# Two unread runs of products lengthened at the start of a softmax attention, and a group's first stack transfers issued ahead of the rows with its maxima

## The chip, the cores and the metric

The kernel runs on one core of one Trainium2 chip. The metric is the device time of one execution in microseconds (us), given as the median of three runs. TensorE is called PE below, VectorE DVE, ScalarE ACT, GpSimd POOL and SyncE SP; SP issues the transfers that this text is about.

## The reference, cut to what matters

One layer is computed: softmax attention, a small feed-forward network, a linear attention over time, and the same network again, each on the layer norm of the running sum. The change touches the first part alone.

```
x:     4 sequences x 512 tokens x 256 channels
mixed  = layernorm(x) @ Wqkv.T         # 16 heads of 16 channels, q, k and v
attn   = softmax(q @ k.T / 4)          # 512 x 512 for each of 4 x 16 pairs
ctx    = attn @ v
x      = x + ctx @ Wproj.T + bproj
```

## The kernel before

The first part works in eight groups: a group is one sequence and half of the heads (8 heads). A group has eight chunks, in two quads: a quad is four heads, and a chunk is one block of 128 keys for the four heads of a quad. PE, ACT and DVE each follow a list of slots written out by hand; slot c of group s is position 8s + c, and there are 70 slots.

What happens to a group, with the lines that do it:

- **Projection.** PE projects q and k of group s + 1 (L373) during slots 1 to 3 of group s. ACT copies the upper parts to `a_dense` (L589) and DVE writes what is left over to it (L679), w = 0 in slot 2 and w = 1 in slot 3.
- **Restacking.** `restack(g, quad)` on SP moves `a_dense` into `a_stack` (L305): three parts, two transfers each, so six transfers of 128 KB a quad. Its first two wait for ACT's copy, the other four for DVE's.
- **Maxima.** PE computes the scores of group s once (L417, four products a slot), and DVE takes each row's negated maximum (L697). After the fourth slot of a quad DVE splits the maxima in two parts, PE turns them (L394, `transpose_max`), ACT copies them (L629), and SP writes them as two more rows of the stack (`rows(g, quad)`, L316, four transfers of 4 KB).
- **Probabilities.** Six slots later PE computes the scores again, turned, with the maxima inside the product (L440, four products a slot), ACT takes the exponentials (L616), and PE multiplies them by the values (L456, `context`). The first L440 of a quad waits for its maxima's rows (`max_rows`), and the first L417 of a quad for its stack (`stacked`).

So in slot c = 4 the maxima of quad 0 of group s are copied, and in slot c = 6 its first L440 needs the rows. In slot c = 0 of the next group the first L417 needs the first quad of that group's stack. SP issues all transfers in the order of its program, and waits at each for what that one needs. The stack has two buffers, so group s + 1 writes where group s - 1 was read.

`unread(count)` on PE (L423) issues products of 128x512 into the accumulator `a_ctx_acc` that nobody reads; the first real product into it starts it afresh. Before the change there are three such runs, all in group 0: six in slot 2, two in slot 4 ahead of `transpose_max`, two in slot 6 ahead of the first L440.

After the softmax part the others follow one after another, so what moves its end moves the end of the kernel.

Of the kernel before, what the change touches and what calls it, by code (L numbers as in the profile page):

```python
# [150 lines left out]
def softmax_attention(nc, semaphore, x, w_qkv, w_stack, loads, bias_rows, x_tok, xn_hi, xn_lo, ident, ctx_tok, norm_tiles):  # L151
# [10 lines left out]
    groups = NB * KD  # L162
# [8 lines left out]
    with ExitStack() as ctx:  # L171
# [111 lines left out]
        @block.sync  # L283
        def _(sp):
            for b in range(NB):
                sp.dma_start(x_tok[:, b * TPB:(b + 1) * TPB, :],
                             x[b].rearrange("(t p) d -> p t d", p=P)).then_inc(x_loaded[b], 16)
                if b == 0:
                    sp.dma_start(stack_raw, w_stack).then_inc(stack_w_loaded, 16)
                    sp.dma_start(w_raw, w_qkv).then_inc(w_qkv_loaded, 16)  # L290
            for dst, src in loads:
                sp.dma_start(dst, src).then_inc(w_loaded, 16)
            sp.wait_ge(set_up, 2)

            def restack(g, quad):

                i, hs = g % 2, slice(quad * 2, quad * 2 + 2)
                if g >= 2:

                    sp.wait_ge(scores_t_done, 4 * ((g - 2) * chunks + (quad + 1) * TPB))  # L300
                for r, (k_part, q_part) in enumerate(((K_HI, Q_HI), (K_LO, Q_HI), (K_HI, Q_LO))):
                    sp.wait_ge(dense_lo_done if r else dense_hi_done, 2 * g + 2)
                    for e in range(2):
                        at, of = e * HALF_ROWS + r * HN, quad * 4 * HN + e * 2 * HN
                        sp.dma_start(f32(stack[i][at:at + HN, hs, :, :]),  # L305
                                     f32(dense[of:of + 2 * HN, i, k_part:q_part + 1:q_part - k_part, :])).then_inc(
                            stacked[i][quad], 16)

            def rows(g, quad):

                i = g % 2
                sp.wait_ge(max_copied, quads * g + quad + 1)
                for e in range(2):
                    for pair in range(2):
                        at, of = e * HALF_ROWS + STACK, (2 * e + pair) * 2 * TPB
                        sp.dma_start(f32(stack[i][at:at + 2, 2 * quad + pair, 1, :]),  # L316
                                     f32(max_rows_t[of:of + 2 * TPB, quad, :])).then_inc(max_rows[quad], 16)

            restack(0, 1)
            for s in range(groups + 1):  # L320
                if s >= 1:
                    rows(s - 1, 1)
                if s < groups:
                    rows(s, 0)
                if s + 1 < groups:
                    restack(s + 1, 0)
                    restack(s + 1, 1)
            sp.wait_ge(w_loaded, 16 * len(loads))

# [26 lines left out]
        def _(pe):  # L356
# [63 lines left out]
            def unread(count):  # L420

                for _ in range(count):
                    pe.matmul(ctx_acc[:], w_hi[:, 0, 0:P], xn_hi[:, 0, 0:SEQ], start=True, stop=True)  # L423

            def probs_chunk(g, c, half):

                quad, t, i = c // TPB, c % TPB, g % 2
                n = g * chunks + c
                if n == 0 and half == 0:
                    unread(2)  # L430
                if t == 0 and half == 0:
                    pe.wait_ge(max_rows[quad], 64 * (g + 1))
                slot = quad * 2 + half
                for e in range(2):
                    q = 4 * n + 2 * half + e
                    if q < TURNS:
                        pe.wait_ge(max_done, last_wide(TURNS + q) + 1)
                    else:
                        pe.wait_ge(probs_done, q - TURNS + 1)
                    pe.matmul(scores_t[q % TURNS][:], half_rows(k_stack[i], e, STACK + 2)[:, slot, t * P:(t + 1) * P],  # L440
                              half_rows(q_stack[i], e, STACK + 2)[:, slot, :], start=True,
                              stop=True).then_inc(scores_t_done, 1)
# [17 lines left out]
            def after_context(s, c):  # L460

                projects, values = s + 1 < groups, s + 1 < groups and (s + 1) % KD == 0
                if c == 0 and s >= 1:
                    if s % KD == 0 and s < groups:
                        pe.wait_ge(v_copied, copied(s))
                    elif turned_in(s - 1):
                        pe.wait_ge(ln.lo_done, KD * (turned_in(s - 1) + 1))
                    else:
                        pe.wait_ge(ctx_done, quads * (s - 2) + 1)
                    transpose_max(s - 1, 1)  # L470
                elif c == 1 and projects:
                    if s >= 2:
                        pe.wait_ge(ctx_done, quads * (s - 1))
                    elif s == 1:
                        pe.wait_ge(max_copied, quads * s)
                    else:
                        pe.wait_ge(v_copied, 1)
                        for e in range(2):
                            project_values(0, 1, e)
                    if s >= 1:  # L480
                        project(s + 1, 0, 0)
                elif c == 0 and s == 0:
                    for k in range(KD):
                        project(0, 1, k)
                    for w in range(2):
                        project_stack(1, w)
                elif c == 3 and projects:
                    project(s + 1, 1, 1)
                elif c == 4 and s < groups:
                    if s == 0:  # L490
                        unread(2)
                    if projects:
                        pe.wait_ge(dense_lo_done, 2 * (s + 1) + 2)
                    else:
                        pe.wait_ge(ctx_done, quads * (s - 1))
                    transpose_max(s, 0)
                elif c == 5 and values:
                    pe.wait_ge(ctx_done, quads * (s - 1) + 1)
                    project_values((s + 1) // KD, 0, 0)
                elif c == 7 and values:  # L500
                    project_values((s + 1) // KD, 1, 1)
                elif c == 5 and turned_in(s):
                    if s >= 1:
                        pe.wait_ge(ctx_done, quads * (s - 1) + 1)
                    else:
                        pe.wait_ge(max_copied, 1)
                    pe.wait_ge(ln.normed, (turned_in(s) + 1) * TPB)
                    ln.turn(pe, turned_in(s), 0, misc)
# [49 lines left out]
            for slot in range(groups * chunks + lag):  # L558
                s, c, n = slot // chunks, slot % chunks, slot - lag
# [1405 lines left out]
```

## Time and profile before

| what | value |
|---|---|
| median of three runs | 1193.58 us (1189.43 to 1196.62) |
| profiled execution, its own time | 1196.9 us |
| its span | 1195.1 us |
| PE busy | 1136.5 us, 95% of the span |
| DVE busy | 930.0 us, 78% |
| ACT busy | 773.7 us, 65% |
| granted clock of PE, mean | 0.975 |

The softmax part takes about the first 276 us of the span. PE's busy share is high, but a product's end is modelled, and at half of the clock the same products are busy for longer. So what counts is where PE stood still, what ended that, and which clock was granted. The granted clock has two levels here: 1.00 is 2.4 GHz and 0.50 is 1.2 GHz.

### The profile page before, as it was taken

What the parts mean: (1) busy time and instruction counts of PE and PEld (TensorE: products, weight loads), DVE (VectorE), ACT (ScalarE), POOL (GpSimd) and SP (SyncE); (2) the same over time, 40 slices, a digit from 0 to 9 for tenths busy, and PEclk for the clock granted to TensorE, in tenths of its full rate; (3) what the DMA queues carried; (4) which work ended last, traced back from release to release, by engine and by line L of the source; (5) the groups of instructions that cost most, each with busy time, mean ns of one, the idle gap of its engine ahead of it and who ended that gap; (6) DMA issues with size and microseconds to landing.
All of it is one profiled execution on the core that took longest, in us unless ns stands there. A gap on an engine that the chain in (4) does not pass through costs nothing. (4 is left out here: it accounts for less than half of the span.)

```text
span 1195.1 us, 22426 instructions
## 1 busy us (share of the span) xinstructions
PE 1136.5 (95%) x7548; PEld 909.1 (76%) x7548; DVE 930.0 (78%) x2126; ACT 773.7 (65%) x1535; POOL 636.8 (53%) x1077
## 2 busy tenths in 40 slices
PE   8899999888898899999999999999999999999768
PEld 7443434336666899999999999999999999999646
DVE  6888877855557988888888888888888888888552
ACT  3377766773456676777776777777777777676423
POOL 4020500000614876777786777686777687767520
PEclk9799989998998999999999999999999999999889
DMA  6434434400320111112111211211211201111020
GB/s 181 55 55 55 55 54 55 54 2 1 113 69 20 34 48 67 47 33 82 34 46 37 78 39 41 76 38 44 71 45 35 82 33 46 33 47 33 16 70 1
DMA packets 23449, 60.50 MB, mean 51 GB/s; under 512 B 3367, under 2 KB 8359, under 8 KB 22183
## 3 DMA queue, kind: packets, MB, share of 16 engines
q1 hardware_dynamic: 23335, 59.07, 19.0%
q8 instruction: 61, 1.00, 0.4%
q14 instruction: 53, 0.43, 0.1%
HBM read 44.67 MB, written 2.33 MB: 39 GB/s over the span
## 5 line engine op out<-in xcount | busy, mean ns | idle before, releaser
L1722 DVE SCALAR_TENSOR_TENSOR ln_xn<-l_proj_q,par,ln_xn 128x511 f32<-128x511 f32 (+2 forms) x192 | 142.4, 742 | 99.4 <-ACT ln_xn L1621 97.1
L697 DVE TENSOR_REDUCE a_neg_max<-a_scores 128x1 f32<-128x512 f32 x244 | 155.1, 683 | 39.9 <-PE a_scores L417 38.1
L616 ACT ACTIVATE a_probs<-a_scores_t 128x512 f32<-128x512 f32 x256 | 138.3, 599 | 65.1 <-PE a_scores_t L440 64.2
L1627 ACT ACTIVATE ln_xn<-ln_xn,par 128x512 f32<-128x512 f32 x128 | 92.6, 724 | 94.0 <-DVE ln_xn L1722 94.0
L1378 POOL TENSOR_TENSOR l_k_tok<-l_normed,k_norm 128x384 f32<-128x384 f32 x64 | 65.2, 1018 | 158.6 <-ACT l_normed L1638 158.6
L1722 DVE SCALAR_TENSOR_TENSOR ln_xn<-l_proj_k,par,ln_xn 128x511 f32<-128x511 f32 (+2 forms) x192 | 142.9, 744 | 4.5
L1638 ACT ACTIVATE l_normed<-l_turn_q,l_shift,l_scale 128x128 f32<-128x128 f32 x256 | 96.5, 457 | 27.2 <-POOL l_shift L1370 27.2
L1368 POOL TENSOR_TENSOR l_scale<-l_small,l_minus_half 128x8 f32<-128x8 f32 x64 | 105.2, 1644 | 5.0
L1638 ACT ACTIVATE l_normed<-l_turn_k,l_shift,l_scale 128x128 f32<-128x128 f32 x256 | 97.4, 481 | 0.0
L1692 ACT ACTIVATE l_gate<-l_proj_gv 128x512 f32<-128x512 f32 x64 | 38.2, 597 | 80.1 <-PE l_proj_gv L1440 80.1
L1576 PE MATMUL l_outp<-l_masked,l_values 128*128 128x128 f32 x512 | 89.3, 277 | 0.1
L1408 POOL TENSOR_TENSOR l_gated_lo<-l_gated,l_gated_hi 128x512 fp32r<-128x512 f32 x64 | 83.3, 1302 | 9.3 <-ACT l_gated_hi L1661 9.3
L1729 DVE TENSOR_TENSOR_SCAN l_decay<-l_keep,ident 128x128 f32<-128x128 f32 x256 | 87.1, 403 | 0.0
L440 PE MATMUL a_scores_t<-a_stack 50*128 50x512 f32 x256 | 76.6, 510 | 9.1 <-ACT a_probs L616 5.0
L96 POOL TENSOR_SCALAR ln_var_eps<-ln_mean_var 128x4 f32<-128x4 f32 (+1 forms) x13 | 3.0, 233 | 152.9 <-DVE ln_mean_var L79 94.2
L440 PEld LDWEIGHTS a_scores_t<-a_stack 50*128 50x128 f32 x256 | 29.9, 192 | 64.9 <-ACT a_probs L616 39.7
L1604 PE MATMUL l_outp<-wo_hi,l_gated_hi 128*128 128x256 f32 x256 | 73.6, 288 | 5.5 <-DVE l_gated L1820 3.4
L1453 PE MATMUL l_proj_gv<-head_hi,xn_hi 128*128 128x256 f32 x256 | 76.5, 299 | 0.3 <-ACT l_gate L1692 0.3
L89 POOL MEMSET ln_minus_half<- 128x4 f32 (+1 forms) x4 | 0.4, 102 | 139.5 <-POOLq L171 139.4
L456 PE MATMUL a_ctx_acc<-a_probs,a_v_tok 128*32 128x512 f32 x512 | 72.5, 640 | 2.3 <-ACT a_probs L616 1.7
L1579 PE MATMUL l_outp<-l_q_late,l_state 128*128 128x128 f32 x384 | 74.5, 276 | 0.0
L1576 PEld LDWEIGHTS l_outp<-l_masked,l_values 128*128 128x128 f32 x512 | 73.3, 194 | 0.3 <-issue 0.3
(347 smaller groups left out, 3614.6 us busy)
## 6 DMA issues: line engine op xcount, KB each, us to landing
l_keep<-keep_rows SPq DMA_DIRECT2D x64, 448.0 KB, 3.6
a_stack<-a_dense SPq DMA_DIRECT2D x90, 128.0 KB, 5.1
head_raw<-w_heads SPq DMA_DIRECT2D x8, 1024.0 KB, 6.7
x_tok<-x SPq DMA_DIRECT2D x4, 512.0 KB, 8.3
wo_raw<-w_o SPq DMA_DIRECT2D x1, 2048.0 KB, 12.0
out<-x_tok SPq DMA_DIRECT2D x1, 1920.0 KB
a_stack<-a_max_rows_t SPq DMA_DIRECT2D x64, 4.0 KB
ctx_tok<-w_qkv SPq DMA_DIRECT2D x1, 768.0 KB, 6.9
```

The source lines that it names most:

```text
L440: pe.matmul(scores_t[q % TURNS][:], half_rows(k_stack[i], e, STACK + 2)[:, slot, t * P:(t + 1) * P], half_rows(q_stack[i], e, STACK + 2)[: ...
L616: act.activation(probs[:, n % 2, h, :], scores_t[(4 * n + h) % TURNS][:], ACT.Exp, scale=SOFT_SCALE).then_inc(probs_done, 1)
L697: dve.tensor_reduce(neg_max[:, g % 2, at:at + 1], max_bank(g, j), AX.X, ALU.max, negate=True).then_inc(max_done, 1)
L1368: pool.tensor_tensor(scale[:, i, :], small[:, 7, :], minus_half[:], ALU.pow).then_inc(scales_ready, 1)
L1408: pool.tensor_tensor(gated_lo[:, k % 4, :], gated[:], f32(gated_hi[:, k % 4, :]), ALU.subtract).then_inc(gated_lo_done, 1)
L1453: last = pe.matmul(proj_gv[:, t * PAIR:(t + 1) * PAIR], lhs, rhs, start=(j == 0), stop=(j == 3 * KD - 1))
L1576: last = pe.matmul(outp[:, tok], values[:, c % 2, t, e * DK:(e + 1) * DK], masked[:, m, tok], start=True, stop=(t == 0))
L1579: last = pe.matmul(outp[:, tok], state[:, m, t - 1, :], q_late[:, m, (t - 1) * P:t * P], start=False, stop=True)
L1627: act.activation(conv[:, w, m, :], conv[:, w, m, :], ACT.Silu, bias=par[:, h, 2 * TAPS + w:2 * TAPS + w + 1]).then_inc(act_sem[w], 1)
L1638: last = act.activation(normed[:, w, t, :], turn[w][:, t * P:(t + 1) * P], ACT.Identity, scale=scale[:, m, j:j + 1], bias=shift[:, m, j:j ...
L1722: ins = dve.scalar_tensor_tensor(conv[:, w, m, s:], proj[w][:, 0:SEQ - s], par[:, h, tap:tap + 1], conv[:, w, m, s:], ALU.mult, ALU.add)
L1729: last = dve.tensor_tensor_scan(decay[:, tok], keep[:, r, tok], ident[:], 0.0, ALU.mult, ALU.add)
```

## The change

The run of two unread products in slot 4 becomes a run of five, and that of two in slot 6 a run of ten. On SP, `restack(s + 1, 0)` of groups s = 1 to 6 is issued ahead of `rows(s, 0)` and no longer behind it. For s = 0 the order is as before. No transfer and no product that is read is added or removed.

```diff
             for s in range(groups + 1):
                 if s >= 1:
                     rows(s - 1, 1)
+                if s >= 1 and s + 1 < groups:
+                    restack(s + 1, 0)
                 if s < groups:
                     rows(s, 0)
+                if s == 0:
+                    restack(1, 0)
                 if s + 1 < groups:
-                    restack(s + 1, 0)
                     restack(s + 1, 1)
...
                 if n == 0 and half == 0:
-                    unread(2)
+                    unread(10)
...
                     if s == 0:
-                        unread(2)
+                        unread(5)
```

On SP the order at s = 1 was this before. `a_stack1<-a_max_rows_t` is `rows(1, 0)`, and `a_stack0<-a_dense` is the stack of group 2, first quad 0 and then quad 1.

```order
L316 DMA a_stack1<-a_max_rows_t 2x4x128 [waits a_max_copied]
L316 DMA a_stack1<-a_max_rows_t 2x4x128 x3
L305 DMA a_stack0<-a_dense 16x2x1024 [waits a_dense_hi_done,a_scores_t_done]
L305 DMA a_stack0<-a_dense 16x2x1024
L305 DMA a_stack0<-a_dense 16x4x512 [waits a_dense_lo_done]
L305 DMA a_stack0<-a_dense 16x4x512
L305 DMA a_stack0<-a_dense 16x4x512 [waits a_dense_lo_done]
L305 DMA a_stack0<-a_dense 16x4x512
```

And this is the same stretch of SP's program in the changed kernel.

```order
L305 DMA a_stack0<-a_dense 16x2x1024 [waits a_dense_hi_done,a_scores_t_done]
L305 DMA a_stack0<-a_dense 16x2x1024
L305 DMA a_stack0<-a_dense 16x4x512 [waits a_dense_lo_done]
L305 DMA a_stack0<-a_dense 16x4x512
L305 DMA a_stack0<-a_dense 16x4x512 [waits a_dense_lo_done]
L305 DMA a_stack0<-a_dense 16x4x512
L316 DMA a_stack1<-a_max_rows_t 2x4x128 [waits a_max_copied]
L316 DMA a_stack1<-a_max_rows_t 2x4x128 x3
```

Six stack transfers now stand between the copy of the dense parts and the four transfers of the rows; the same swap recurs for each s up to 6.

On PE the first lengthened run stood as follows, in slot 4 of group 0 ahead of the turning of the maxima (L394).

```order
L417 MATMUL a_scores_t1<-a_stack0 128x512 [waits a_max_done,a_stacked01]
L417 MATMUL a_scores_t2<-a_stack0 128x512 [waits a_max_done]
L417 MATMUL a_scores0<-a_stack0 128x512 [waits a_max_done]
L417 MATMUL a_scores1<-a_stack0 128x512 [waits a_max_done]
L423 MATMUL a_ctx_acc<-xn_hi,a_w_hi 128x512 x2
L394 MATMUL a_misc<-ident,a_max_parts 32x128 [waits a_max_split,a_dense_lo_done]
```

In the changed kernel three lines more stand ahead of `unread` in the file, and the count is five.

```order
L420 MATMUL a_scores_t1<-a_stack0 128x512 [waits a_max_done,a_stacked01]
L420 MATMUL a_scores_t2<-a_stack0 128x512 [waits a_max_done]
L420 MATMUL a_scores0<-a_stack0 128x512 [waits a_max_done]
L420 MATMUL a_scores1<-a_stack0 128x512 [waits a_max_done]
L426 MATMUL a_ctx_acc<-xn_hi,a_w_hi 128x512 x5
L397 MATMUL a_misc<-ident,a_max_parts 32x128 [waits a_max_split,a_dense_lo_done]
```

Only the run itself has grown; the run of ten grows in the same way ahead of the first L440.

## Rows read from the trace of the kernel before

**Rows 1.** The page: granted clock of PE in 40 slices of the span
```profile
PEclk9799989998998999999999999999999999999889
```

**Rows 2.** Windows: stretch, its length, busy us (instructions), PEclk, DMA share, GB/s
```profile
40.71:54.36 13.65, 12.71 (x45) 5.41 (x46) 9.48 (x18) 6.18 (x13) 0.00 (x0) 0.50 0.88 117
170.42:177.24 6.82, 6.82 (x28) 2.85 (x24) 3.67 (x7) 2.44 (x5) 0.00 (x0) 0.50 0.28 33
```

**Rows 3.** Timeline of PE, group 0: start, us, instruction [idle before <-releaser]
```profile
30.34 1.65 PE L423 MATMUL a_ctx_acc<-xn_hi,a_w_hi 128*128 128x512 f32 x6
...
37.13 0.28 PE L394 MATMUL a_misc<-ident,a_max_parts 128*32 128x128 f32 x1 [1.05 <-DVE a_dense L679]
...
39.17 0.71 PE L423 MATMUL a_ctx_acc<-xn_hi,a_w_hi 128*128 128x512 f32 x2
41.66 0.80 PE L440 MATMUL a_scores_t<-a_stack 50*128 50x512 f32 x2 [1.77 <-DMA a_stack<-a_max_rows_t]
...
50.02 1.21 PE L417 MATMUL a_scores<-a_stack 48*128 48x512 f32 x2
...
54.37 0.96 PE L440 MATMUL a_scores_t<-a_stack 50*128 50x512 f32 x2
```

**Rows 4.** Timeline, group 2, the stretch from its rows to its stack
```profile
96.63 0.60 ACT L589 ACTIVATE a_dense<-a_misc 128x512 fp32r<-128x512 f32 x1
...
98.88 2.57 SPq L316 DMA_DIRECT2D a_stack<-a_max_rows_t  x4
...
102.69 0.42 PE L440 MATMUL a_scores_t<-a_stack 50*128 50x512 f32 x1
...
103.31 0.50 PE L440 MATMUL a_scores_t<-a_stack 50*128 50x512 f32 x1 [0.20 <-ACT a_probs L616]
...
108.86 0.40 PE L440 MATMUL a_scores_t<-a_stack 50*128 50x512 f32 x1
...
109.93 0.67 PE L417 MATMUL a_scores<-a_stack 48*128 48x512 f32 x2
```

**Rows 5.** Timeline of PE, group 2, the slots behind that
```profile
113.01 0.50 PE L440 MATMUL a_scores_t<-a_stack 50*128 50x512 f32 x2
...
117.33 0.50 PE L440 MATMUL a_scores_t<-a_stack 50*128 50x512 f32 x2
```

**Rows 6.** Timeline of PE, group 4, the same slots as in group 2
```profile
167.00 0.39 PE L440 MATMUL a_scores_t<-a_stack 50*128 50x512 f32 x1
...
169.10 0.50 PE L417 MATMUL a_scores<-a_stack 48*128 48x512 f32 x2 [0.99 <-DMA a_stack<-a_dense]
...
179.06 0.50 PE L440 MATMUL a_scores_t<-a_stack 50*128 50x512 f32 x2
```

**Rows 7.** Timeline of SP's queue: runs of twelve stack transfers (two quads)
```profile
40.50 7.65 SPq L305 DMA_DIRECT2D a_stack<-a_dense  x12
...
159.68 8.68 SPq L305 DMA_DIRECT2D a_stack<-a_dense  x12
```

**Rows 8.** Timeline, group 6: rows issued with nothing of the stack ahead
```profile
218.74 2.57 SPq L316 DMA_DIRECT2D a_stack<-a_max_rows_t  x4
...
222.47 0.61 PE L440 MATMUL a_scores_t<-a_stack 50*128 50x512 f32 x2 [0.24 <-DMA a_stack<-a_max_rows_t]
```

**Rows 9.** Timeline, group 6 to 7: rows issued behind twelve stack transfers
```profile
229.79 0.50 PE L417 MATMUL a_scores<-a_stack 48*128 48x512 f32 x2 [0.57 <-DMA a_stack<-a_dense]
...
231.83 2.65 SPq L316 DMA_DIRECT2D a_stack<-a_max_rows_t  x4
...
236.03 0.50 PE L440 MATMUL a_scores_t<-a_stack 50*128 50x512 f32 x2 [0.76 <-DMA a_stack<-a_max_rows_t]
```

**Rows 10.** Timeline, group 1: the same chain in an odd group
```profile
67.05 0.60 ACT L589 ACTIVATE a_dense<-a_misc 128x512 fp32r<-128x512 f32 x1
...
69.29 2.55 SPq L316 DMA_DIRECT2D a_stack<-a_max_rows_t  x4
...
74.43 0.51 PE L440 MATMUL a_scores_t<-a_stack 50*128 50x512 f32 x2
```

## The prediction

> **What bounds the kernel now.** I read the granted clock over the whole span first. The page's line of the clock stays at 9 tenths but for a few slices, and the second is one of them, near the place of the lengthened runs [rows 1]. The windows then give the two stretches of the softmax part that matter here. From 40.71 to 54.36 us PE ran at 0.50 of its clock (1.2 GHz) for 13.65 us, and from 170.42 to 177.24 for 6.82 us; it was busy for 12.71 and 6.82 us of them, so these are stretches of work at half speed [rows 2].
>
> Next I read what PE did just before each. Before the first it stood still for 1.05 us ahead of the turning of the maxima and for 1.77 us ahead of the first L440, which waited for the rows of the maxima [rows 3]. Before the second it stood still for 0.99 us at the first L417 of group 5, which waited for its stack [rows 6]. A shorter wait of that kind, 0.57 us, opens group 7, and did not lower the clock [rows 9].
>
> Last I read the slack of the two kinds of transfers that trade places. In group 6 the four transfers of the rows are issued from 218.74 for 2.57 us, to 221.31, and the L440 that waits for them starts at 222.47: **they land 1.16 us after the end of their issue** [rows 8]. In group 2 the issue ends at 101.45 and the L440 starts at 102.69, 1.24 us later, so there they land with no slack [rows 4]. In group 1 the issue ends at 71.84, they land at 73.0, and L440 starts at 74.43: 1.4 us of slack [rows 10]. Groups 4 and 6 repeat group 2 and groups 3 and 5 repeat group 1. The stack has as little: in group 2 the issue of the rows ends at 101.45, the stack follows, and the first L417 starts at 109.93, about when it lands; the same wait cost 0.99 and 0.57 us two and four groups later [rows 4, 6, 9]. So at both places a transfer sets when PE goes on, and SP can serve only one first.
>
> **The longer runs.** Six unread products took 1.65 us, some 0.25 from one to the next once the tail of the last is left off [rows 3]. Three more in slot 4 are 0.75 us inside a wait of 1.05: they cost nothing, and if DVE were earlier by more than 0.3 us they would show. Eight more in slot 6: ten products from 39.17 at 0.25 take PE's issue to 41.67, and the rows let L440 go at 41.66 [rows 3]. I put the cost at 0.1 us; the bounds are nothing, and 0.25 us, one product. What they give is the clock: PE then works through both waits that came before the first fall, and I expect no fall there.
>
> What is that worth? From 41.66 to 54.37 are three slots, 12.71 us [rows 3]. The same three slots of group 2, 102.69 to 113.01, took 10.32 at 1.00, and hold one run of L456 more (about 1.0 us), so 9.3 [rows 4, 5]. But the full 3.4 us can't come back. The stack of group 1 is issued from 40.50, and in group 2 one issued from 101.45 let its L417 go at 109.93, 8.4 us later [rows 7, 4]. So the L417 that starts group 1 at 50.02 can't start before 48.9: 1.1 us. From there to the end of the slot it took 4.35 us (50.02 to 54.37) against 3.1 (109.93 to 113.01): 1.25 us. **Gain: 2.4 us**, between 0 (a fall at the new wait for that stack) and 3.4.
>
> **The swap on SP.** In groups 1 to 6 SP now starts on the stack when ACT has copied the dense part. Twelve such transfers are issued in 7.65 us, 0.64 each, or in 8.68 where the queue paused; the seven such runs lie between these two [rows 7]. Six take 3.8 us, then the rows 2.57, then 1.16 to land: 7.6 us from ACT's copy. Their own condition, the copy of the maxima, is met meanwhile (SP could start them at 98.88, 1.65 us after ACT's copy ended) [rows 4].
>
> - Even groups (2, 4, 6): ACT's copy ends at 97.23, so the rows land at 104.8 where L440 started at 102.69. **PE waits 2.1 us** [rows 4]. Three times: 6.3.
> - Odd groups (1, 3, 5): 67.65 + 7.6 = 75.25 against 74.43. **PE waits 0.8 us** [rows 10]. Three times: 2.4.
> - The pauses of the queue: up to 1.0 us more in a run of twelve [rows 7]. I take 0.2 a group, 1.2; bounds 0 and 2.4.
> - What comes back: behind the L440 that would wait, the next product starts 0.62 us after the first since it waits for ACT's exponentials, where 0.25 is the pace without a wait [rows 3, 4]. After a stall ACT has caught up, and the 0.4 us is not paid; the pair that begins at 108.86 waits in the same way. I take 0.6 us in each even group, 1.8, between 1.2 and 2.4. In the odd groups PE has no such waits, and nothing comes back.
> - The stack lands some 4 us earlier, so the waits of 0.99 and 0.57 us go: 1.6 gained [rows 6, 9]. The fall of the clock that followed the first goes too. It cost: 167.00 to 179.06 is 12.06 us, the same slots of group 2, 108.86 to 117.33, are 8.47; of the 3.6 us the wait is 1.0. **A fall of the clock costs 2.6 us**, and one is gained [rows 4 to 6].
> - New falls: the new waits of 2.1 us are longer than each of those before the two falls in rows (1.05 with 1.77, and 0.99), and 0.57 and 0.76 were followed by none [rows 2, 3, 6, 9]. So I expect the odd groups to keep the clock and the even ones to lose it mostly: two falls of three, 5.2 us; bounds 0 and 7.8.
>
> Who waits behind? On SP the second quad's stack follows, 1.7 us earlier than before, so nobody. On PE all of the slot waits, and ACT and DVE with it once they have done what is ready; hence the stall counts in full but for what came back above.
>
> The size hangs on one thing more. In rows 9 four transfers of rows were issued behind twelve of the stack, to 234.48, and let L440 go at 236.03, 1.55 us after and not 1.16 [rows 8, 9]. The Trainium skill, page "DMA: Bandwidth & Descriptors", section on queues, rings and completion order, says that on each DMA engine descriptors are taken in the order of the ring. By that the small rows must wait for the big transfers ahead of them to drain, and the 0.4 us agrees in sign.
>
> **The sum.** 0.1 + 6.3 + 2.4 + 1.2 - 1.8 - 1.6 - 2.6 + 5.2 - 2.4 = **+6.8 us**. Against the profiled execution's 1196.9 that is 1203.7. The median of the runs is 3.3 us lower than that execution, so on its scale the forecast is 1193.6 + 6.8 = 1200.4.
>
> **The rivals.**
> - *The clock holds.* The waits for the rows come as computed, but no fall follows them: 6.8 - 5.2 = +1.6 us, 1195.2. For it speaks that PE is busy on both sides of each wait; against it that 0.99 us was enough once.
> - *The queue holds the rows back.* If the rows land only after the sixth stack transfer, they come 8.4 us after its first issue and not 7.6; with that 0.8 us in six groups (4.8), and a third fall (2.6), it is +14.2, 1207.8. Rows 9 show 0.4 of it.
> - *Faster: the rows' wait is absorbed.* The wait replaces waiting that PE has later in the same group, for ACT and for the stack. In the even groups the two waits for ACT are 0.8 us and that for the stack up to 1.0; should the rows land 1.8 us or less after their old place, an even group loses nothing and an odd one nothing up to its 1.4 us. It then takes the stack to be issued faster, or DVE and ACT to set the pace. The gains are left: 2.4 + 2.6 + 1.6 = 6.6 us, 1187.0. From a landing 5.9 us after ACT's copy (odd groups 6.8), not 7.6, it decides.
> - *The runs don't keep the clock.* The first fall comes a little later, at the new wait for group 1's stack: +2.4 on the forecast, 1202.8.
>
> **How the numbers follow.** A measurement of this kernel can tell about 0.5% (6 us) from no change; its three runs spread over 7.2 us. Chances: forecast 0.40 (alone 1197 to 1205), clock holds 0.20, queue holds back 0.13, absorbed 0.20, first fall stays 0.07. Slower by more than 0.5% is above 1199.5: half and a little more of the forecast, all of the queue's case and most of the last, and some of the clock's, 0.45. Faster is under 1187.6: somewhat more than half of the absorbed case, with some from the clock's when another fall later is missing, 0.19. The rest is 0.36. The range of 1188 to 1208 leaves out half of the absorbed case and the upper half of the queue's.
>
> **What would show it.** Right: the runs of five and ten stand close to L397 and L443, and the clock is 1.00 from 37 to 48 us; in groups 1 to 6 the stack's first transfers start within 0.1 us of ACT's copy and the rows' issue 3.8 us later; L443 has waits for the rows of about 2 and 1 us in turn, no L420 waits for the stack but the first of group 1; stretches of 0.50 follow the even groups' waits. Wrong: the rows' waits are under 0.5 us; or they are there and the end of the softmax part has still moved forward; or the falls come at other places, so that their number is chance and the medians differ by it.

## The result, and the profile after

| | before | changed |
|---|---|---|
| median of 4 runs each | 1191.51 us (1186.12 to 1196.62) | 1217.74 us (1216.2 to 1226.04) |
| profiled execution, its own time | 1196.9 us | 1226.04 us |
| its span | 1195.1 us | 1224.2 us |
| granted clock of PE, mean | 0.975 | 0.955 |

The ratio is 1.023 with a 95% interval of 1.0171 to 1.0288. The kernel became slower by 26 us, where +6.8 was forecast; the time lies outside the range. The sign was right, the size was not. The profiled execution of the changed kernel is the slowest of its four and 8.3 us above their median, so the stretches at half clock below may add up to more than in the other three, which were not profiled.

The page of the changed kernel, its line of the clock and the row of its scores (the last number is the idle time that the rows of the maxima ended). What was L440 is now L443, L417 is L420, and L394 is L397.

```profile
PEclk9888899968899899999999999999999999999979
...
L443 PE MATMUL a_scores_t<-a_stack 50*128 50x512 f32 x256 | 80.6, 544 | 20.6 <-DMA a_stack<-a_max_rows_t 16.4
```

The line of the clock answers to [rows 1]. A slice is 30.6 us. In the softmax part, now ten slices long, the second to the fifth stand at 8 tenths, the ninth at 6 and the tenth at 8; in its nine slices before, the second stood at 7, the sixth at 8 and the rest at 9. PE's waits in 36 to 310 us say what was late (total us, times, longest):

```profile
PE a_scores_t L443 <- DMA a_stack<-a_max_rows_t: 16.4, 8, 3.7
...
PE a_scores L420 <- DMA a_stack<-a_dense: 1.3, 1, 1.3
```

In the same stretch before, the wait for the rows was 4.0 us in five. Here is one group after another, groups 1, 2 and 6 of the changed kernel, in the timeline. It answers to [rows 10, 4, 8].

```profile
65.61 0.61 ACT L592 ACTIVATE a_dense<-a_misc 128x512 fp32r<-128x512 f32 x1
...
66.29 3.80 SPq L305 DMA_DIRECT2D a_stack<-a_dense  x6
...
70.13 2.65 SPq L316 DMA_DIRECT2D a_stack<-a_max_rows_t  x4
...
74.91 0.49 PE L443 MATMUL a_scores_t<-a_stack 50*128 50x512 f32 x2 [1.85 <-DMA a_stack<-a_max_rows_t]
...
100.09 0.60 ACT L592 ACTIVATE a_dense<-a_misc 128x512 fp32r<-128x512 f32 x1
...
100.76 3.96 SPq L305 DMA_DIRECT2D a_stack<-a_dense  x6
...
104.77 2.66 SPq L316 DMA_DIRECT2D a_stack<-a_max_rows_t  x4
...
109.19 0.50 PE L443 MATMUL a_scores_t<-a_stack 50*128 50x512 f32 x2 [2.88 <-DMA a_stack<-a_max_rows_t]
...
236.35 0.60 ACT L592 ACTIVATE a_dense<-a_misc 128x512 fp32r<-128x512 f32 x1
...
245.75 0.80 PE L443 MATMUL a_scores_t<-a_stack 50*128 50x512 f32 x2 [3.66 <-DMA a_stack<-a_max_rows_t]
```

Read each as one chain. In group 2 ACT's copy ends at 100.69, SP starts at 100.76, the six stack transfers take 3.96 us, the rows 2.66, and the L443 that needs them starts 1.76 us after the end of their issue. From ACT's copy to L443 that is 8.5 us, in group 1 it is 8.7 (with 2.13 behind the issue), in group 6 8.8. The trace also has the moments of landing. In group 2 the sixth stack transfer lands at 108.58 and the rows at 109.15, and in all of groups 1 to 6 the rows land 0.6 to 0.8 us after that sixth transfer. The six waits of groups 1 to 6 are 1.85, 2.88, 1.93, 3.09, 1.67 and 3.66 us, 15.1 in all.

The windows of the changed kernel at half clock in that part (columns as in [rows 2], to which they answer), and the one ahead of the first:

```profile
36.00:49.49 13.49, 11.27 (x60) 5.65 (x59) 12.52 (x23) 6.57 (x13) 0.00 (x0) 1.00 0.67 92
49.49:56.31 6.82, 6.82 (x26) 2.73 (x24) 4.01 (x9) 2.34 (x5) 0.00 (x0) 0.50 0.47 56
76.79:83.62 6.83, 6.83 (x28) 3.50 (x26) 2.75 (x5) 2.95 (x7) 0.00 (x0) 0.50 0.45 60
110.93:127.99 17.06, 17.06 (x62) 6.59 (x64) 10.54 (x22) 7.66 (x15) 0.00 (x0) 0.50 0.19 26
148.47:155.30 6.83, 6.83 (x28) 3.59 (x28) 2.79 (x5) 2.99 (x7) 2.70 (x1) 0.50 0.41 49
182.61:189.43 6.82, 6.82 (x29) 2.74 (x25) 3.78 (x8) 3.74 (x8) 0.00 (x0) 0.50 0.52 72
244.05:264.53 20.48, 18.78 (x70) 6.81 (x70) 9.78 (x18) 8.38 (x17) 0.00 (x0) 0.50 0.27 40
```

Each from the second on begins 1.5 to 1.9 us behind the end of a wait for the rows (74.91, 109.19, 146.62, 181.14), the last already within it (ended 245.75); only group 5's wait, 1.67 us, has none behind it. Together they are 64.8 us at 0.50, against the 20.5 of [rows 2].

How the two traces drift apart is seen from the first scores product of each group's probabilities:

| group | 1 | 2 | 3 | 4 | 5 | 6 | 7 |
|---|---|---|---|---|---|---|---|
| before, us | 74.43 | 102.69 | 132.57 | 160.82 | 194.29 | 222.47 | 248.17 |
| changed, us | 74.91 | 109.19 | 146.62 | 181.14 | 214.15 | 245.75 | 277.39 |
| difference | 0.5 | 6.5 | 14.1 | 20.3 | 19.9 | 23.3 | 29.2 |
| changed, waits filled, us | 75.56 | 107.11 | 138.17 | 169.71 | 200.62 | 232.05 | 256.49 |

The last row belongs to an experiment below. The spans of the first two differ by 29.1 us, so all of it arises in the softmax part. Groups 2, 3, 4, 6 and 7 each lose 3 to 8 us on the one before; in the step to group 5 the kernel before lost its own fall [rows 6], and nothing is added.

At the place of the longer runs the timeline of PE (group 0, answers to [rows 3]) reads

```profile
36.42 0.29 PE L397 MATMUL a_misc<-ident,a_max_parts 128*32 128x128 f32 x1 [0.36 <-DVE a_dense L682]
...
38.45 2.56 PE L426 MATMUL a_ctx_acc<-xn_hi,a_w_hi 128*128 128x512 f32 x10
40.94 0.50 PE L443 MATMUL a_scores_t<-a_stack 50*128 50x512 f32 x2
...
48.16 0.50 PE L420 MATMUL a_scores<-a_stack 48*128 48x512 f32 x2 [1.33 <-DMA a_stack<-a_dense]
```

The wait ahead of the turning shrank from 1.05 to 0.36 us, the one ahead of L443 is gone, and the clock stays at 1.00 to 49.49. Then it falls, behind a new wait of 1.33 us for group 1's stack.

### The profile page after: what moved, and what is told of

It is laid out like the page before. It is cut to its first block and busy times, and to the rows that moved or that the text cites. A ratio compares the mean times of both kernels' runs of the same rounds, so it can differ in the third digit from the quotient of the medians.

```text
span 1224.2 us, 22448 instructions
## 1 busy us (share of the span) xinstructions
PE 1155.1 (94%) x7559; PEld 918.2 (75%) x7559; DVE 930.9 (76%) x2126; ACT 773.2 (63%) x1535; POOL 635.4 (52%) x1077
## 5 line engine op out<-in xcount | busy, mean ns | idle before, releaser
L443 PE MATMUL a_scores_t<-a_stack 50*128 50x512 f32 x256 | 80.6, 544 | 20.6 <-DMA a_stack<-a_max_rows_t 16.4
L443 PEld LDWEIGHTS a_scores_t<-a_stack 50*128 50x128 f32 x256 | 31.5, 205 | 81.8 <-ACT a_probs L619 36.7
L459 PE MATMUL a_ctx_acc<-a_probs,a_v_tok 128*32 128x512 f32 x512 | 79.6, 698 | 2.1 <-ACT a_probs L619 1.7
L1463 PEld LDWEIGHTS l_scores<-l_qk 128*128 128x128 f32 x512 | 68.3, 195 | 6.3 <-issue 1.5
```

The lines of the kernel that those rows point to most:

```text
L459: last = pe.matmul(ctx_acc[e * SLOT:(e + 1) * SLOT, :], v_tok[g % 4][:, t, quad * 4 + e, :], probs[:, n % 2, e, :], start=(t == 0), stop=( ...
```

## The experiments

The open questions were three: which half of the change costs; why the rows land 8.5 to 8.8 us after ACT's copy and not 7.6; and how much of the loss is waiting and how much is the clock. The edits are shown against the changed kernel. Each time stands beside that of the kernel before on the same chip, which is 1189.67 to 1191.9 us. Line numbers differ by a few from kernel to kernel, so the names say what an instruction is.

### The swap alone, and the runs alone

```diff
-                    unread(10)
+                    unread(2)
...
-                        unread(5)
+                        unread(2)
```

> The swap on SP alone, with the unread runs of two as before. If the loss is the swap's (rows of the maxima landing 8.5 us after ACT's copy of the dense part, and the clock falling behind the waits), this is at least as slow as the changed kernel: 24 to 30 us above before, PE's waits for the rows 15 to 17 us in total, and 40 us or more of softmax time at 0.50 of the clock in groups 1 to 6. The fall near 41 us is there again. If the longer unread runs had a share in the loss (by shifting where the clock falls), it is 5 us or more faster than the changed kernel.

Measured: 1223.57 us against 1191.02, a ratio of 1.0287 (1.0245 to 1.0329). PE's waits in 36 to 310 us:

```profile
PE a_scores_t L443 <- DMA a_stack<-a_max_rows_t: 18.7, 8, 3.7
```

The other half is the changed kernel with SP's old order.

```diff
-                if s >= 1 and s + 1 < groups:
-                    restack(s + 1, 0)
                 if s < groups:
                     rows(s, 0)
-                if s == 0:
-                    restack(1, 0)
                 if s + 1 < groups:
+                    restack(s + 1, 0)
```

> The runs of five and ten alone, with SP's order as before. My account: no fall of the clock near 41 us; the wait moves to the first L417 of group 1 (about 1.3 us), where the clock may fall for 6.8 us; net 0 to 2.4 us faster than before, so 'same' within what can be told. Rival (the longer runs delay the first L440 and what follows): 1 to 3 us slower, L440 of group 0 starts more than 0.5 us after the end of the rows' landing.

Measured: 1190.91 against 1191.02, 1.0002 (0.9981 to 1.0024). Its windows:

```profile
40.00:48.81 8.81, 7.03 (x40) 3.19 (x42) 7.83 (x15) 5.71 (x11) 0.00 (x0) 1.00 0.94 131
48.81:59.05 10.24, 10.24 (x35) 3.87 (x27) 5.82 (x12) 3.43 (x7) 0.00 (x0) 0.50 0.37 45
```

The whole loss is the swap's. The swap alone is even 5.8 us above the changed kernel (1223.57 and 1217.74), but the two ran on different chips and the intervals of their ratios overlap, so a gain of the longer runs beside the swap isn't shown by this. In its trace the waits for the rows in groups 1 to 6 are 2.17, 3.04, 1.99, 3.42, 1.70 and 3.67 us, and 3.41, 10.24, 6.83, 3.41, none and 34.13 us at 0.50 belong to them. The longer runs hold the clock at 1.00 through 40 to 48.81 us, where it was 0.50 before, and then the fall comes anyway, behind a 1.35 us wait for group 1's stack. In this profiled execution it is moved, not removed, and the time doesn't change.

### How many stack transfers may stand ahead

`restack` was given the parts to issue, so that two or four of the six go ahead of the rows and the rest behind.

```diff
                 if s >= 1 and s + 1 < groups:
-                    restack(s + 1, 0)
+                    restack(s + 1, 0, (0,))
                 if s < groups:
                     rows(s, 0)
                 if s == 0:
                     restack(1, 0)
+                elif s + 1 < groups:
+                    restack(s + 1, 0, (1, 2))
```

With four ahead the parts are (0, 1) and (2,).

> As the changed kernel, but only the first two of the six stack transfers of a group's first quad go ahead of the rows, the other four behind. They fit in the 1.65 us between ACT's copy of the dense part and ACT's copy of the maxima. If the rows are late because SP issues them late or because the ring in front of them is full (both theories agree here), they are not late now: PE's waits for the rows under 1 us each, no long run of half clock in groups 1 to 3, the waits for the stack at the start of groups 5 and 7 gone, 2 to 6 us faster than before. If any stack transfer ahead of the rows holds them up (a transfer's fixed cost and not the data), waits of 1 us or more stay in the even groups and it is slower than before.

> Four of the six stack transfers ahead of the rows. By the issue alone the rows land 4 x 0.64 + 2.57 + 1.16 = 6.3 us after ACT's copy of the dense part; by the ring (rows behind all data ahead of them, first transfer 3.2 us and 1.0 for each further one, and some 0.4) 6.6 us. So odd groups have no wait for the rows and even ones one of 0.8 to 1.2 us. Time: between two_ahead and the changed kernel, within 6 us of before; nearer to before the fewer falls of the clock there are (each counts 2.6 us).

Measured: two ahead 1185.81, 0.9963 (0.9942 to 0.9984); four ahead 1197.83, 1.0052 (1.0027 to 1.0077), both against 1191.02. Timeline of group 2, two ahead:

```profile
93.63 0.60 ACT L596 ACTIVATE a_dense<-a_misc 128x512 fp32r<-128x512 f32 x1
...
94.31 1.33 SPq L307 DMA_DIRECT2D a_stack<-a_dense  x2
...
95.87 2.62 SPq L318 DMA_DIRECT2D a_stack<-a_max_rows_t  x4
...
99.70 0.45 PE L447 MATMUL a_scores_t<-a_stack 50*128 50x512 f32 x1
```

And four ahead:

```profile
94.14 3.02 SPq L307 DMA_DIRECT2D a_stack<-a_dense  x4
...
97.20 2.65 SPq L318 DMA_DIRECT2D a_stack<-a_max_rows_t  x4
...
101.04 0.50 PE L447 MATMUL a_scores_t<-a_stack 50*128 50x512 f32 x2 [1.34 <-DMA a_stack<-a_max_rows_t]
```

With two ahead the L447 starts 5.5 us after ACT's copy and has no wait; with four it is 7.0 us (the copy ended at 94.07), and PE waits 1.34; in groups 4 and 6 it is 6.6, with waits of 0.94 and 1.42. The sign turns between 5.5 and 7.0, where the prediction had set the point of decision for the even groups at 5.9. In both, L447 starts 1.2 us after the end of the rows' issue, as in [rows 8]. Among these kernels the extra time behind the issue, 1.8 to 2.2 us, is there only with six ahead. With two ahead the clock is 1.00 from 42 to 275 us in the profiled execution, although PE waits 1.33 us for group 1's stack there as well.

### The same waits with PE kept at work

In groups 1 to 6 the changed kernel issues more unread products just where it would wait for the rows, into a bank that the next scores product overwrites.

```diff
+                if t == 0 and half == 0 and quad == 0 and 1 <= g <= 6:
+                    pe.wait_ge(probs_done, 4 * n - TURNS + 1)
+                    for _ in range(8 if g % 2 else 13):
+                        pe.matmul(scores_t[4 * n % TURNS][:], w_hi[:, 0, 0:P], xn_hi[:, 0, 0:SEQ], start=True, stop=True)
```

> The changed kernel with unread products issued ahead of each late wait for the rows in groups 1 to 6 (8 in the odd groups, 13 in the even ones, into the bank that the next L443 overwrites), so that PE works through the wait. The rows are as late as before this edit. If the part of the loss beyond the waits themselves is the clock's, no stretch at 0.50 follows the rows' waits in groups 1 to 6 and the kernel comes down from 1217.7 by 12 to 18 us, to about 1200 to 1206, that is 9 to 15 us above before. If the half clock is a mark of the waits and costs little beyond them (DVE and ACT set the pace then), it stays above 1212.

Measured: 1200.86 against 1190.93, 1.0088 (1.0054 to 1.0122). PE's timeline in group 2:

```profile
103.94 3.24 PE L437 MATMUL a_scores_t<-xn_hi,a_w_hi 128*128 128x512 f32 x13
107.11 0.50 PE L447 MATMUL a_scores_t<-a_stack 50*128 50x512 f32 x2
```

Window of its softmax part:

```profile
57.40:270.00 212.60, 201.91 (x1192) 92.13 (x1190) 162.66 (x302) 143.06 (x284) 21.23 (x13) 1.00 0.31 46
```

PE gets no further than with a wait, since the products fill the time, yet the clock is 1.00 all the way from 57.40 us. The first L447 of a group starts 8.6 to 8.8 us after ACT's copy and at most 0.3 after the rows have landed, so the unread products cost next to nothing of their own. That splits the loss: **9.9 us are what the late rows cost with the clock held (1200.86 - 1190.93; the gains of the change are already taken off), and 16.9 are the clock (1217.74 - 1200.86)**. The sum, 26.8, agrees with the 26.2 of the change itself. In the traces the same two steps are 8.3 and 20.9 us up to group 7, by the table of the groups above; another 5.1 us of the clock's step arise behind the softmax part, where the profiled execution of the changed kernel has four more stretches at 0.50 before 415 us (23.9 us) and this one has one (3.4 us).

### Is it the queue, the issue or the data?

ACT issues the rows of groups 1 to 6 on its own queue, while SP issues the stack.

```diff
-                if s < groups:
+                if s in (0, groups - 1):
                     rows(s, 0)
...
+                if quad == 0 and 1 <= g <= groups - 2:
+                    act.wait_ge(max_copied, quads * g + quad + 1)
+                    for e in range(2):
+                        for pair in range(2):
+                            at, of = e * HALF_ROWS + STACK, (2 * e + pair) * 2 * TPB
+                            act.dma_start(f32(stack[g % 2][at:at + 2, 2 * quad + pair, 1, :]),
+                                          f32(max_rows_t[of:of + 2 * TPB, quad, :])).then_inc(max_rows[quad], 16)
```

> The changed kernel, but ACT issues the rows of quad 0 of groups 1 to 6 right behind its own copy of the maxima, on its own queue, while the six stack transfers stand ahead on SP's queue. If the rows are late because of SP's order of issue and of the queue that they share with the stack, they land about 1.2 to 1.5 us after their issue ends, and PE's waits for the rows are under 1 us each. If the DMA engines are simply full (the data ahead has to move first whatever the queue), the first L443 of the even groups still starts 8.5 us after ACT's copy of the dense part, with waits of 2 to 3 us. ACT loses some 2.6 us a group to issuing, so PE may wait for exponentials instead; the total time is not the test here.

Measured in one profiled execution, without an interval: 1227.11 us. Its timeline in group 2:

```profile
101.07 0.60 ACT L592 ACTIVATE a_dense<-a_misc 128x512 fp32r<-128x512 f32 x1
...
101.75 11.42 SPq L305 DMA_DIRECT2D a_stack<-a_dense  x12
...
103.32 2.58 ACTq L638 DMA_DIRECT2D a_stack<-a_max_rows_t  x4
...
105.94 2.06 ACT L619 ACTIVATE a_probs<-a_scores_t 128x512 f32<-128x512 f32 x4 [2.65 <-issue]
...
110.25 0.50 PE L443 MATMUL a_scores_t<-a_stack 50*128 50x512 f32 x2 [0.69 <-DMA a_stack<-a_max_rows_t]
```

What SP's queue itself waited for, 60 to 260 us (total us, times, longest):

```profile
SPq L305 <- PE a_scores_t L443: 31.2, 6, 7.0
```

The rows were issued by 105.90, and L443 still started at 110.25, 4.35 us later and 8.6 after ACT's copy, where it also stood with SP issuing. In groups 1 to 6 they land 8.3 to 8.5 us after ACT's copy, in five of the six 0.2 to 0.3 us after the sixth stack transfer and in group 3 0.5 us before it. A queue of their own gave the small rows no way past the large transfers. The Trainium skill, page "DMA: Bandwidth & Descriptors", section "Issuing engines are not separate DMA queues", says that transfers of every issuing engine run on the same 16 engines and interleave; the 4.35 us agree. ACT also stands for 2.65 us while it issues, so PE now waits for exponentials (15.7 us in all) and for the rows only at the end: the 0.69 us here isn't the 2 to 3 us that was expected. The 11.42 us of SP's twelve transfers are no slower issue. Six are issued at the usual pace, then SP waits until PE has finished with the stack that the other six overwrite, as the view of its waits says.

The counter-test keeps SP's order and count but moves almost no data: six transfers of 1 KB in DRAM take the place of the six of the stack ahead of the rows.

```diff
                 if s >= 1 and s + 1 < groups:
-                    restack(s + 1, 0)
+                    sp.wait_ge(dense_hi_done, 2 * (s + 1) + 2)
+                    for n in range(6):
+                        sp.dma_start(small[s, n:n + 1, :], x[0][n:n + 1, :]).then_inc(small_moved, 16)
                 if s < groups:
                     rows(s, 0)
```

(`restack(s + 1, 0)` stands behind the rows again.)

> SP's order as before, but with six transfers of 1 KB (from the input to a scratch area that nobody reads) ahead of the rows in groups 1 to 6, where the changed kernel has the six stack transfers. It costs SP's queue the issue and puts no data ahead. By the step of my prediction (issue alone), the first L443 of a group starts 7.6 us after ACT's copy of the dense part, with waits of about 0.8 us in the odd and 2.1 us in the even groups. By the other theory (the data of the stack has to move first) the issue explains only part of the 8.5 to 8.8 us of the changed kernel: here 7.6 or less, so that 0.9 us or more a group is the data's. If the issue of small transfers is as slow as their landing and the start comes at 8.5 us here too, the data has no part. The stack comes later than before, so PE also waits for it at the start of the next groups; the total time is not the test.

Measured in one profiled execution, without an interval: 1221.67 us. Timeline, the start of groups 1 and 2 of the probabilities:

```profile
64.16 0.60 ACT L595 ACTIVATE a_dense<-a_misc 128x512 fp32r<-128x512 f32 x1
...
64.79 3.77 SPq L328 DMA_DIRECT2D a_small<-x  x6
...
68.61 2.68 SPq L318 DMA_DIRECT2D a_stack<-a_max_rows_t  x4
...
72.45 0.50 PE L446 MATMUL a_scores_t<-a_stack 50*128 50x512 f32 x2 [0.84 <-DMA a_stack<-a_max_rows_t]
...
103.47 0.79 PE L446 MATMUL a_scores_t<-a_stack 50*128 50x512 f32 x2 [2.58 <-DMA a_stack<-a_max_rows_t]
```

L446 starts 7.7 us after ACT's copy (64.76 to 72.45), and so it does in groups 3, 4 and 6; in groups 2 and 5 it is 8.2, since SP's queue paused by 0.4 to 0.5 us during the issue. The waits are 0.84, 0.80 and 1.35 in odd groups, 2.58, 2.04 and 2.53 in even ones. Where the queue didn't pause, 7.6 us is the prediction's own number, and the waits are near its 0.8 and 2.1. From the end of the rows' issue to L446 it is 1.2 to 1.3 us in every group, against 1.8 to 2.2 in the changed kernel. **Issue and plain landing are 7.7 us, and the stack's transfers ahead add 0.8 to 1.1.** Whether their bytes or the number of their packets does it isn't separated, since the small ones have less of both. But the total is as bad as the change's, and the windows say why:

```profile
103.19:123.67 20.48, 20.20 (x74) 7.42 (x76) 11.50 (x23) 8.75 (x17) 0.00 (x0) 0.50 0.59 79
171.45:191.93 20.48, 20.06 (x74) 7.28 (x74) 10.94 (x20) 8.75 (x17) 0.00 (x0) 0.50 0.58 78
239.72:273.85 34.13, 33.34 (x120) 11.83 (x121) 17.85 (x33) 15.84 (x32) 0.00 (x0) 0.50 0.36 47
```

A fall stands at each even group's wait of 2.0 to 2.6 us and none at the odd ones of 0.8 and 1.35. The forecast had this pattern, but a fall lasts 20 to 34 us here.

### A version faster than both, and what each part of it is worth

Two ahead, now in group 0 too, so that the stack of group 1 comes earlier.

```diff
-                if s >= 1 and s + 1 < groups:
-                    restack(s + 1, 0)
+                if s + 1 < groups:
+                    restack(s + 1, 0, (0,))
                 if s < groups:
                     rows(s, 0)
-                if s == 0:
-                    restack(1, 0)
+                if s + 1 < groups:
+                    restack(s + 1, 0, (1, 2))
```

> As two_ahead, with the first two stack transfers ahead of the rows in group 0 as well. There they fit in the 2.4 us between ACT's copy of the dense part and that of the maxima. The stack of group 1 lands 1.3 us earlier, so the 1.3 us wait at its first L424 goes, and with it the last wait of over 1 us in the groups: 1 to 1.5 us faster than two_ahead, 0.4 to 0.7% faster than before, no stretch at 0.50 before 250 us. If the wait for group 1's stack is set by something else (DVE's copy of the rest, the second quad's transfers), no difference from two_ahead.

Measured: 1182.92 against 1190.93, 0.9928 (0.9901 to 0.9954). The same with the old runs of two and two:

> The order of two_ahead_all with the unread runs of two and two as in the kernel before. It tells what the longer runs are worth once no transfer is late. If they keep the clock, this one has the fall near 41 us again (6.8 us or more at 0.50) and is 1.5 to 3.4 us slower than two_ahead_all, near 1185. If the runs are worth nothing (the fall's cost is hidden behind the wait for group 1's stack), the two are within 1 us.

Measured: 1186.88 against 1191.9, 0.9956 (0.9937 to 0.9975). These two had run on different chips, so both ran again on one.

> The same kernel as two_ahead_all, as the base of the other two kernels of this call on the same chip: 0.5 to 0.9% faster than before, 1181 to 1185 us.

> The same kernel as two_all_short2, now on the same chip as its counterpart with the longer unread runs. If the longer runs keep the clock to good effect, it is 1.5 to 4 us slower than two_all_again; if the difference of before was that of the chips, within 1 us.

Measured, both against 1189.67: with the long runs 1182.13, 0.9944 (0.9917 to 0.9971); with the short ones 1186.93, 0.9975 (0.9952 to 0.9997). Window of the long one:

```profile
36.00:270.00 234.00, 216.76 (x1288) 95.38 (x1288) 183.01 (x342) 163.90 (x324) 21.31 (x14) 1.00 0.33 49
```

Window of the short one:

```profile
37.72:47.96 10.24, 9.66 (x34) 4.63 (x33) 8.56 (x15) 4.44 (x9) 0.00 (x0) 0.50 0.64 94
```

With long runs and an early stack there is no fall from 36 to 270 us; with the short runs there is one of 10.24, and two of 3.41 between 259 and 274 us. Here the runs are worth 4.8 us by the medians (1186.93 - 1182.13), more than the 1.5 to 4 expected, where with the old order they gave 0.1. The traces say how much of that is the fall near 38 us: group 1 starts at 69.52 with the long runs and at 72.27 with the short ones, 2.8 us apart, and group 7 at 238.43 and 241.24, still 2.8. The other 2 us arise behind that, where the two executions differ in their later falls, and aren't assigned.

### One group alone with six ahead

The version above, but in group 2 all six go first.

```diff
-                    restack(s + 1, 0, (0,))
+                    restack(s + 1, 0, (0, 1, 2) if s == 2 else (0,))
...
-                    restack(s + 1, 0, (1, 2))
+                    restack(s + 1, 0, () if s == 2 else (1, 2))
```

> The order of two_ahead_all (two stack transfers ahead of the rows everywhere), but all six ahead in group 2 alone: one late landing of the rows, one wait of 2.5 to 3 us in an even group, in a kernel whose clock otherwise holds. It prices one event. If a fall of the clock costs 2.6 us as I had it, this is 5 to 6 us above two_ahead_all of the same chip; if a fall behind an even group's wait lasts 17 us and more, as in the changed kernel, and costs 5 to 8 us by itself, it is 8 to 11 us above; if the clock holds after a single wait, 2.5 to 3.

Measured: 1186.18 against 1189.67, 0.9968 (0.9948 to 0.9987), which is 4.05 us over the version without it on the same chip and between the cases that were set out. Its timeline, group 2:

```profile
101.81 0.50 PE L445 MATMUL a_scores_t<-a_stack 50*128 50x512 f32 x2 [2.92 <-DMA a_stack<-a_max_rows_t]
```

Its windows:

```profile
102.92:109.74 6.82, 6.82 (x30) 2.42 (x24) 4.12 (x7) 3.65 (x8) 0.00 (x0) 0.50 0.52 68
109.74:256.00 146.26, 138.32 (x827) 59.71 (x823) 119.54 (x224) 105.15 (x209) 15.09 (x7) 1.00 0.31 45
256.51:283.82 27.31, 23.10 (x86) 9.60 (x85) 4.47 (x9) 12.90 (x24) 0.10 (x1) 0.50 0.00 1
```

One late landing, one fall, and then the clock stays up to 256 us. There a stretch of 27.31 us at 0.50 begins, at a wait of 1.01 us for the rows of group 7's second quad; the version above has the same wait at 250.52, and its clock stays at 1.00. This profiled execution, 1197.49 us, is the slowest of thirteen and 11.3 above their median, so it serves for the groups before 256 us and not for the kernel's time. From the first scores product of group 1 to that of group 2 it took 31.37 us against 28.25 in the version above, the wait; from group 2 to 3, 31.60 against 29.84, the fall less what comes back after the stall. From group 3 to 7 the two agree within 0.1 us. So 3.1 and 1.8 us, 4.9 together, where the medians differ by 4.05.

## Why the prediction was right or wrong

**The longer runs** (+0.1, and -2.4 for the first fall). Their cost was right: L443 starts at 40.94 with no wait. That they hold the clock through the two waits was right too. The gain didn't come: the fall moved 8 us, to the wait for group 1's stack. That wait was in the working (the L417 can't start before 48.9; it started at 48.16), and so was the fall as a lower bound and as a rival, "the runs don't keep the clock", with 0.07. The runs alone measured 1.0002. Where that wait is gone too, they are worth 2.8 us up to group 7 and 4.8 by the medians; the 2.4 of the sum was a fair price for the fall, and the place where it would come back was wrong.

**The landing of the rows** (7.6 us after ACT's copy). Of the sum, 3.8 + 2.57 for the issue was right; 1.16 for what follows was not. It was taken from a row with nothing of the stack ahead [rows 8], while [rows 9] already showed 1.55 behind twelve. With the six stack transfers ahead it is 1.8 to 2.2. The small transfers brought the 7.6 back but for the queue's pauses, and the queue of ACT did not. This is the rival "the queue holds the rows back", 8.4 in its working against 8.5 to 8.8 measured. Its cause holds but for the word queue: what holds them back is the stack's transfers on the shared engines, whichever queue the rows come from, and they land with or just after the sixth.

**The waits** (6.3 + 2.4 + 1.2, -1.8 for what comes back, -1.6 for the stack). The six waits are 15.1 us where these terms have 9.9 for them. The stack's waits at groups 5 and 7 are gone, as said. With the clock held from 57 us on, the forecast's terms are +4.0 (6.6 - 2.6, without the gain of the first fall, which that kernel still has), and the run with filled waits measured +9.9. The missing 5.9 is the late landing. With the waits filled the first L447 stands 8.7 us after ACT's copy, against 5.4 in the even groups and 6.8 in the odd ones before, that is 3.3 and 2.0 later and 15.8 in all, where the forecast had 9.9. The 1.8 of what comes back held. From group 2 to 3 the filled kernel takes 31.06 us against 29.88 before, 1.2 more, while its rows are 2.0 late in group 3, so 0.8 came back behind group 2, where 0.6 was forecast.

**The clock** (5.2 for two falls, -2.6 for one gained). This is the step that failed most: "two falls of three, 5.2 us; bounds 0 and 7.8". Two things were wrong in it. The number: falls followed five of the six waits, the odd groups' 1.85 and 1.93 us too, since these were not 0.8. And the length: the price was read from one stretch of 6.82 us [rows 2, 6], and stretches of 17.06 and 20.48 us came, 20.48 and 34.13 with the small transfers. The new falls cost 16.9 us where the sum had 5.2 for them. The price of a short one held. From group to group the changed kernel takes 2.7, 3.0 and 2.1 us longer than the one with filled waits where a stretch of 6.8 us lies between, 6.4 with the 17.06 and 7.2 with the 20.48.

**The account.** The sum missed 19.4 us: 11.7 in the falls (16.9 for 5.2), 5.9 in the late landing, 2.4 in the first fall that wasn't gained. That is 20.0, and the other 0.6 is what the two differences of medians have over the change itself.

**The faster rival** had its point of decision about right, 5.9 us in an even group. The change misses it by 2.6; two transfers ahead, at 5.5, meet it, and four, at 6.6 to 7.0, do not. The gains that it named were real as well: its 6.6 us stand against 8.0 and 7.5 measured for the best version.

**What stays open** is what sets the length of a stretch. The same wait of about 2.9 us was followed by 17.06 us in the changed kernel and by 6.82 in the one with a single group of six; 2.58 us was followed by 20.48 with the small transfers, and 3.42 by 3.41 in the kernel with the swap alone. Whether a wait near 1.3 us lowers the clock at all is as open: the wait for group 1's stack did so in four profiled kernels with the longer runs and not in three (two ahead, four ahead, small transfers). In the kernel with four ahead single executions differ by 10 us (1190.28 to 1200.47), and its profiled one, the fastest, shows next to none of the falls in this part (one of 3.41 us); so part of this varies from execution to execution, and a difference between two single profiles doesn't settle it.

## What to carry to other kernels

Price a transfer that is moved behind others by a row in which as much data stands ahead of it, not by its issue alone: six transfers of 128 KB ahead cost a 4 KB one 1 us beyond their issue, on the same queue or another. Where a wait that repeats is long enough to lower PE's clock, don't take one stretch at half clock for the length of all, and count a fall at each repetition; filling such waits with unread products shows in one run what the waiting itself costs. When a fall is taken away at one place, look for the next wait of that length behind it: the runs alone gave 0.1 us, and with the next wait gone too 4.8. And before a profile is read for a kernel's time, set its own time beside the median: two of the profiles here were 8 and 11 us above it.

## What the runs showed of the hardware that was not expected

- Waits of PE of 1.85 to 3.67 us for the rows, in a part where PE was else busy, each had a stretch at 0.50 (1.2 GHz) with them, fourteen of fourteen in four traces, of 3.41 to 34.13 us. Between 0.9 and 1.8 us both came. Among others, 0.99 (before), 1.33 and 1.35 (group 1's stack in four kernels) and 1.42 (four ahead) were followed by one; 1.29, 1.33 and 1.38 (group 1's stack in three kernels), 1.34 (four ahead), 1.35 (small transfers), 1.67 and 1.70 (group 5, changed kernel and swap alone) were not.
- While the clock was at 0.50, PE was busy for nearly the whole stretch (17.06 of 17.06 us, 18.78 of 20.48, 33.34 of 34.13), so the fall outlived its wait by far.
- With six large transfers on SP's queue, four of 4 KB on ACT's took 4.35 us from the end of their issue until PE could go on, against 1.16 with nothing ahead [rows 8]; on SP's queue behind the six it was 1.8 to 2.2, and in both cases they landed 8.3 to 8.8 us after ACT's copy, close to the sixth.
- With two of the six stack transfers ahead the rows were not late at all: 5.5 us after ACT's copy in group 2, as before the change.
